# Attention and mixture-of-experts block: one sequence for the score maxima of all units, head-block subtraction on GpSimd

## Chip, cores and metric

The kernel runs on one core of one Trainium2 chip. The metric is device time of one launch in microseconds (us), given as the median of the runs.

## What is computed

The input x has 4 sequences of 2048 rows of 256. It is layer-normalised to xn; the output is x plus two branches of xn.

```python
x = x + attn(xn) + ffn(xn)
# attn: per row, 16 heads of 16 attend to each other (16 x 16 scores a row)
score = jnp.einsum('bsid,bsjd->bsij', Q, K) / jnp.sqrt(jnp.float32(D_K))
attn = jax.nn.softmax(score, axis=-1)
# ffn: causal latent attention over 2048 positions, 16 heads of 16, then top-2 of 8 experts
c = h @ Wdkv
scores = jnp.einsum('bqhd,bkhd->bhqk', q, k) / jnp.sqrt(...)
scores = jnp.where(causal, scores, -1e9)
a = jax.nn.softmax(scores, axis=-1)
out = jnp.einsum('bhqk,bkhd->bqhd', a, v)
```

The first branch is cheap and has no matrix shape: it is done on VectorE and GpSimd in blocks of 128 rows, the "head blocks". The second is the causal attention of this case, then the experts.

## The kernel before

Five stages run one after the other: projections (phase1_project), causal attention (phase2_attend), routing, experts, and the combination. The change is in phase2_attend alone.

**Units and steps.** The attention has 16 units (`UNITS`), each of four heads of one sequence. A unit goes through 40 steps (`STEPS`, L675): for each of four chunks of 512 queries the key tiles of 128 up to the diagonal. In a step TensorE computes transposed scores of two pairs of heads into two PSUM buffers (`scores`, L1109, with masks on the diagonal by `add_mask`, L144), ScalarE takes their exponentials (`exps`, L1036), and two steps later (`LAG`) TensorE multiplies them with the values (`values`, L1127). At the end of a chunk ScalarE copies the result out (`copy_pv`, L1049). On the diagonal a step covers only 384, 256 or 128 of the 512 queries.

**Maxima.** A softmax over transposed scores needs each row's maximum beforehand. It enters the scores as two more rows of the query tile. So while unit n is attended, TensorE also computes the untransposed scores of unit n+1 piece by piece (`score_pair`, L1078, masks L144) into a ring of three PSUM banks, and VectorE reduces every piece to its maximum (`reduce_item`, L971). A pair is two pieces, one of each half of the heads, and takes two banks; a unit has 72 pairs, 144 reductions. A piece is 512 wide in most pairs, 384 in eight, and two heads of 128 or of 256 together in eight. TensorE issues a pair once two banks are free. After the last pair VectorE reduces the piece maxima to negated row maxima (`reduce_maxima`, L978), TensorE transposes them (`transpose_max`, L1092), VectorE splits them in two bf16 parts (`split_maxima`, L986, L988), and SyncE stores them into the next unit's query tile (`store_neg_rows`, L94), which the scores of step 0 wait for.

**Order of work.** It is written out by hand, one program per engine. `PAIRS_BY` says how many pairs are issued by the end of each step: it shares them over steps 0 to 34 by cost, the last `AHEAD` = 5 steps have none, and the last unit has none at all. Per step the pairs are 2 2 2 1 | 3 2 2 2 3 1 2 1 | 3 2 2 2 2 3 2 2 2 2 1 2 | 2 2 2 2 3 2 2 2 2 2 3 0 0 0 0 0 (a bar ends a chunk). In a step TensorE issues both scores, half of the pairs, the values, then the other half. The transpose comes in step 36.

**Head blocks.** GpSimd weighs two head blocks a unit (`weigh_heads`, products at L905, sums at L911, L917, result L924), loads the next two, scores them (`score_heads`, L890 to L898), and divides one tile of attention results by the softmax sums (`divide`, L938). Of each block VectorE takes the maximum and subtracts it (`shift_heads`, L998 and L1000), at steps 12 and 20 (`SHIFT_AT`); ScalarE takes the exponential two steps later (L1043), which `weigh_heads` waits for. VectorE also inverts the sums at step 10 (L993). Semaphores keep each engine's order, so an engine that waits holds all behind it in its program.

**Loads.** There are three slots of unit tiles. SyncE loads unit n+2 in 26 parts, two a step of its own list, each waiting for a later `values` of unit n (up to step 24).

Of the kernel before, what the change touches and what calls it, by code (L numbers as in the profile page):

```python
# [665 lines left out]
def phase2_attend(nc, apart, qk_heads, v_units, o, head_qkv, attn_rows, first_units):  # L666
# [23 lines left out]
    PAIRS_BY = [sum(sum(pair_cost[:m + 1]) * sum(step_cost) <= sum(step_cost[:i + 1]) * sum(pair_cost)  # L690
                    for m in range(N_PAIR)) for i in range(N_STEP)]
    assert PAIRS_BY[N_STEP - AHEAD - 1] == N_PAIR

    with ExitStack() as ctx:
# [14 lines left out]
        piece_max = sb("p2_piece_max", [P, HG, KT, NC])  # L709
# [48 lines left out]
        SHIFT_AT = (12, 20)  # L758
# [7 lines left out]
        N_ITEM = 2 * N_PAIR + 1  # L766
        assert SLOTS * N_ITEM % RING == 0

        MAX_ITEM = N_ITEM - 1

        def ring_item(n, s, r):

            return N_ITEM * n + r, (N_ITEM * s + r) % RING

        def units(eng, body):

            for n in range(UNITS):
                body(n, n % SLOTS, (n - 1) // SLOTS, (n - 1) % SLOTS, n + 1 < UNITS)

        def first(n):  # L780
            return isinstance(n, int) and n == 0

        def next_round(j, k):

            return j + (k + 2) // SLOTS

        @block.sync
        def _(sp):
            def store_neg_rows(n, s):
                wait_apart(sp, ring_free, RING + ring_item(n - 1, 0, MAX_ITEM)[0] + 1, apart)  # L790
                store_neg(sp, q6[s], neg_hi, neg_lo, neg_stored)
# [63 lines left out]
        def _(pool):  # L855
# [7 lines left out]
            nc.gpsimd.memset(piece_max[:, :, :, :], -3e38).then_inc(consts, 1)  # L863
# [23 lines left out]
            def score_heads(m, u, loads, before):  # L887

                wait_apart(pool, head_loaded[u], 16 * loads, apart)
                step(nc.gpsimd.tensor_tensor(  # L890
                    terms[:, :, :, :], head_in[:, u, 0, :, :].unsqueeze(2).to_broadcast([P, H, H, DH]),
                    head_in[:, u, 1, :, :].unsqueeze(1).to_broadcast([P, H, H, DH]), ALU.mult), before + 1)
                width = DH // 2
                for k in range(STEPS_A - 1):
                    step(nc.gpsimd.tensor_tensor(terms[:, :, :, 0:width], terms[:, :, :, 0:width],  # L895
                                                 terms[:, :, :, width:2 * width], ALU.add), before + 2 + k)
                    width //= 2
                nc.gpsimd.tensor_tensor(head_s[:, u, :, :], terms[:, :, :, 0], terms[:, :, :, 1], ALU.add  # L898
                                        ).then_inc(head_scored, 1)
                wait_apart(pool, head_scored, m + 1, apart)  # L900

# [47 lines left out]
            with pool.Fori(1, UNITS - 1) as n:  # L949
                body(n)  # L950
                divide(n - 1)
            for u in range(2):
# [6 lines left out]
        def _(dve):  # L959
# [7 lines left out]
            def reduce_item(m, half, g, bank):  # L967
                h, heads, (i, pc, width) = PAIRS[m]
                h += half * PAIR
                dve.wait_ge(ring_filled, g + 1)  # L970
                nc.vector.tensor_reduce(piece_max[:, h:h + heads, i, pc],  # L971
                                        ring_ps[bank][:, 0:heads * width].rearrange("p (h k) -> p h k", h=heads), AX_X,
                                        ALU.max).then_inc(ring_free, 1)

            def reduce_maxima(n, last_item):

                dve.wait_ge(ring_free, RING + last_item + 1)
                nc.vector.tensor_reduce(neg_max[:, 0:HG * KT], piece_max[:, :, :, :].rearrange("p h i c -> p (h i) c"), AX_X, ALU.max, negate=True  # L978
                                        ).then_inc(neg_max_done, 1)

            def split_maxima(n, g, bank):

# [3 lines left out]
                nc.vector.tensor_copy(neg_hi[:, :], ring_ps[bank][0:HG * KT, 0:P]).then_inc(neg_hi_done, 1)  # L986
                dve.wait_ge(neg_hi_done, n + 1)
                nc.vector.tensor_tensor(neg_lo[:, :], ring_ps[bank][0:HG * KT, 0:P], neg_hi[:, :], ALU.subtract  # L988
# [6 lines left out]
            def shift_heads(m, u):  # L995
# [8 lines left out]
            def body(n, s, j, k, has_next):  # L1004
                done = 0
                for i in range(N_STEP):
                    if i in SHIFT_AT:
                        u = SHIFT_AT.index(i)
                        shift_heads(2 * n + u, u)
                    if i == INVERSE_AT and not first(n):  # L1010
                        invert_sums(n - 1)
                    upto = PAIRS_BY[i] if has_next else 0
                    for m in range(done, upto):
# [4 lines left out]
                    done = upto  # L1018
                    if has_next and i == N_STEP - AHEAD + 1:
                        split_maxima(n + 1, *ring_item(n, s, MAX_ITEM))  # L1020
            units(dve, body)

        @block.scalar
        def _(act):
# [26 lines left out]
            def body(n, s, j, k, has_next):  # L1051
                for i in range(N_STEP):
                    if i - 2 in SHIFT_AT:
                        u = SHIFT_AT.index(i - 2)
# [7 lines left out]
            units(act, body)  # L1062

        @block.tensor
        def _(pe):
            def score_pair(s, m, rnd, g, bank):

                h, heads, (i, pc, width) = PAIRS[m]
                banks = [ring_ps[(bank + half) % RING] for half in range(2)]
                if m == 0:  # L1070
                    pe.wait_ge(loaded[s], N_LOAD * (rnd + 1))
# [17 lines left out]
            def transpose_max(n, g, bank):  # L1089
                pe.wait_ge(neg_max_done, n + 1)  # L1090
                pe.wait_ge(ring_free, g + 1)
                nc.tensor.transpose(ring_ps[bank][:, 0:P], neg_max[:, :], ident[:, :]).then_inc(ring_filled, 1)  # L1092
# [41 lines left out]
            def body(n, s, j, k, has_next):  # L1134
                def maxima(first, end):

                    for m in range(first, end):
                        score_pair((s + 1) % SLOTS, m, next_round(j, k), *ring_item(n, s, 2 * m))

                done = 0  # L1140
                for i in range(N_STEP):
                    scores(n, s, i, 0)
                    scores(n, s, i, 1)
                    upto = PAIRS_BY[i] if has_next else 0
# [5 lines left out]
                    done = upto  # L1150
                    if has_next and i == N_STEP - AHEAD + 1:
                        transpose_max(n + 1, *ring_item(n, s, MAX_ITEM))
                for i in range(N_STEP - LAG, N_STEP):
                    values(n, s, i)
            units(pe, body)
# [909 lines left out]
```

## Time and profile before

| | us |
|---|---|
| median of three runs (3166.71 to 3174.38) | 3169.0 |
| the profiled execution | 3161.7 |
| its span in the profile | 3160.2 |

| engine | busy us | share of the span |
|---|---|---|
| TensorE | 2568.8 | 81% |
| VectorE | 2379.8 | 75% |
| GpSimd | 2236.2 | 71% |
| ScalarE | 1543.0 | 49% |

The profile calls TensorE PE and its weight loads PEld, VectorE DVE, ScalarE ACT, GpSimd POOL; L971 is line 971 of the kernel. A timeline row gives start and length in us, the engine, the line, the operation with output and input, and after x how many instructions were merged; in brackets stands the idle time before it and what ended it. A row by stretches gives the stretch, its length, then busy time and (x) instructions of PE, PEld, DVE, ACT and POOL, the granted clock of TensorE, the DMA share and GB/s. A row by groups gives busy time, mean ns of one, and the idle time before. The attention stage runs from 461 to 2086 us of the span.

### The profile page before, as it was taken

To read this page: it belongs to the slowest core of one execution; us is meant where nothing else is said; L and a number is where in the kernel's file an instruction comes from. 1 tells how busy PE (TensorE), PEld (TensorE's weight loads), DVE (VectorE), ACT (ScalarE), POOL (GpSimd) and SP (SyncE) were. 2 spreads that over 40 slices of the span, in tenths; PEclk is the share of its full clock that TensorE was granted. 3 is DMA by queue.
4 is the path that set the end of the run, shared out by engine and by line. 5 is a ranking of instruction groups with operands and counts; after the bars stand their busy time and mean duration, and the time that the engine had idled before them with its cause. 6 is when DMAs were issued, how large, how long until landed. Compare 5 with 4: busy or idle time off the path is not lost. (4 is left out here: it accounts for less than half of the span.)

```text
span 3160.2 us, 60322 instructions
## 1 busy us (share of the span) xinstructions
PE 2568.8 (81%) x21392; PEld 1318.1 (42%) x21392; DVE 2379.8 (75%) x3812; ACT 1543.0 (49%) x2314; POOL 2236.2 (71%) x1193
## 2 busy tenths in 40 slices
PE   7969978899989998899989998948749888999600
PEld 4534432333233333333233333217638777777500
DVE  4447759888988889888988889305657999999334
ACT  2222216666666666667666666822214444444200
POOL 4433339889888988888888988946746656666376
PEclk9979989999999999999999999977759999999855
DMA  6996542232322233222322220147756666666686
GB/s 195 201 299 200 171 145 63 51 75 80 85 72 62 77 83 78 56 81 79 82 62 75 80 81 24 33 140 245 237 192 220 208 201 201 207 211 206 210 248 203
DMA packets 346974, 435.68 MB, mean 138 GB/s; under 512 B 40859, under 2 KB 276861, under 8 KB 346749
## 3 DMA queue, kind: packets, MB, share of 16 engines
q1 hardware_dynamic: 300796, 350.81, 38.5%
q0 software_dynamic: 17920, 54.55, 5.4%
q10 hardware_dynamic: 28032, 27.27, 2.5%
q8 instruction: 147, 2.41, 0.3%
q14 instruction: 79, 0.64, 0.1%
HBM read 273.43 MB, written 158.47 MB: 137 GB/s over the span
## 5 line engine op out<-in xcount | busy, mean ns | idle before, releaser
L971 DVE TENSOR_REDUCE p_piece_max<-p_ring 128x1 f32<-128x512 f32 (+3 forms) x2160 | 1279.4, 653 | 163.2 <-PE p_ring L144 110.7
L1036 ACT ACTIVATE p_probs<-p_st 128x1024 f32<-128x1024 f32 (+3 forms) x1280 | 1076.7, 894 | 497.6 <-PE p_st L1109 295.6
L1109 PE MATMUL p_st<-unit_q,unit_k 64*128 64x512 bf16 (+3 forms) x3520 | 419.1, 348 | 16.5 <-POOL p_minus_one L869 11.5
L905 POOL TENSOR_TENSOR p_terms<-p_head_p,p_head_in 128x4096 f32<-128x4096 f32 x32 | 347.4, 10856 | 102.0 <-ACT p_head_p L1043 101.7
L1127 PE MATMUL p_pv<-p_probs,unit_vg 128*32 128x512 f32 (+3 forms) x3520 | 409.9, 542 | 0.0
L1739 POOL TENSOR_TENSOR p_pv<-p_pr,p_qkv 128x4096 f32<-128x4096 f32 x32 | 347.4, 10857 | 37.0 <-ACT p_pr L1837 36.4
L1078 PE MATMUL p_ring<-unit_k,unit_q 64*128 64x512 bf16 (+3 forms) x1600 | 273.1, 355 | 101.2 <-DVE p_piece_max L971 100.0
L1910 PE MATMUL p_y_ps<-p_w,p_hid 128*128 128x256 f32 x1152 | 284.1, 403 | 27.6 <-ACT p_hid L1850 27.5
L890 POOL TENSOR_TENSOR p_terms<-p_head_in 128x4096 f32<-128x4096 f32 x32 | 283.0, 8844 | 7.6 <-POOL p_head_s L898 4.4
L1897 PE MATMUL p_hid_ps<-p_rT,p_w 128*128 128x256 f32 x1152 | 263.4, 382 | 3.3 <-issue 2.2
L911 POOL TENSOR_TENSOR p_terms<-p_terms 128x2048 f32<-128x2048 f32 (+2 forms) x96 | 252.7, 2632 | 17.1 <-POOL p_terms L911 11.4
L895 POOL TENSOR_TENSOR p_terms<-p_terms 128x2048 f32<-128x2048 f32 (+2 forms) x96 | 252.0, 2625 | 17.1 <-POOL p_terms L895 11.4
L1910 PEld LDWEIGHTS p_y_ps<-p_w,p_hid 128*128 128x128 f32 x1152 | 227.6, 203 | 66.7 <-ACT p_hid L1850 34.3
L1078 PEld LDWEIGHTS p_ring<-unit_k,unit_q 64*128 64x128 bf16 x1600 | 70.8, 93 | 432.9 <-DVE p_piece_max L971 427.0
L1897 PEld LDWEIGHTS p_hid_ps<-p_rT,p_w 128*128 128x128 f32 x1152 | 219.9, 192 | 35.9 <-issue 5.5
L1109 PEld LDWEIGHTS p_st<-unit_q,unit_k 64*128 64x128 bf16 x3520 | 139.7, 95 | 197.3 <-ACT p_probs L1036 92.2
L1109 PE MATMUL p_st<-p_q,p_k 34*128 34x512 bf16 (+7 forms) x1600 | 188.2, 346 | 0.0
L1127 PE MATMUL p_pv<-p_probs,p_vg 128*32 128x512 f32 (+3 forms) x1600 | 186.3, 542 | 0.0
L1969 POOL DMA_INDIRECT p_ye<-expert_rows,p_pos x128 | 132.6, 1036 | 72.2 <-issue 71.9
L1078 PE MATMUL p_ring<-p_k,p_q 64*128 64x512 bf16 (+3 forms) x800 | 135.6, 352 | 49.7 <-DVE p_piece_max L971 49.1
L1775 DVE TENSOR_TENSOR p_prod<-p_q_ps,p_qkv 128x4096 f32<-128x4096 f32 x32 | 141.5, 4421 | 32.1 <-ACT p_q_ps L1830 32.1
L1384 POOL DMA_INDIRECT sorted_rows<-p_th,p_pos x128 | 134.0, 1047 | 37.5 <-issue 36.3
(194 smaller groups left out, 3603.8 us busy)
## 6 DMA issues: line engine op xcount, KB each, us to landing
p_w<-ffn_w SPq DMA_DIRECT2D x144, 512.0 KB, 5.1
qk_parts<-p_parts SPq DMA_DIRECT2D x64, 384.0 KB, 3.2
head_qkv<-p_heads SPq DMA_DIRECT2D x16, 1536.0 KB, 6.7
p_rows<-sorted_rows SPq DMA_DIRECT2D x72, 256.0 KB, 4.2
expert_rows<-p_y ACTq DMA_DIRECT2D x72, 256.0 KB, 5.6
unit_q<-qk_parts SPq DMA_DIRECT2D x132, 128.0 KB, 3.2
unit_k<-qk_parts SPq DMA_DIRECT2D x132, 128.0 KB, 3.6
p_x<-attn_x SPq DMA_DIRECT2D x32, 512.0 KB, 5.7
```

Of the source, the lines that this page charges most:

```text
L890: step(nc.gpsimd.tensor_tensor(terms[:, :, :, :], head_in[:, u, 0, :, :].unsqueeze(2).to_broadcast([P, H, H, DH]), head_in[:, u, 1, :, :]. ...
L895: step(nc.gpsimd.tensor_tensor(terms[:, :, :, 0:width], terms[:, :, :, 0:width], terms[:, :, :, width:2 * width], ALU.add), before + 2 + k)
L905: step(nc.gpsimd.tensor_tensor(terms[:, :, :, :], head_p[:, u, :, :].unsqueeze(2).to_broadcast([P, H, DH, H]), head_in[:, u, 2, :, :].rear ...
L911: step(nc.gpsimd.tensor_tensor(terms[:, :, :, 0:width], terms[:, :, :, 0:width], terms[:, :, :, width:2 * width], ALU.add), before + 2 + k)
L971: nc.vector.tensor_reduce(piece_max[:, h:h + heads, i, pc], ring_ps[bank][:, 0:heads * width].rearrange("p (h k) -> p h k", h=heads), AX_X ...
L1036: nc.scalar.activation(probs[:, 2 * turn_of(s, i) + u, :, 0:width], st_ps[u][:, :, 0:width], ACT.Exp).then_inc(probs_done, 1)
L1078: last[half] = nc.tensor.matmul(banks[half][:, k * width:(k + 1) * width], q6[s][rows, h + k, i * P:(i + 1) * P], k6[s][rows, h + k, pc * ...
L1109: last = nc.tensor.matmul(st_ps[u][:, half, 0:width], k6[s][rows, PAIR * second + u, kt * P:(kt + 1) * P], q6[s][rows, PAIR * second + u, ...
L1127: last = nc.tensor.matmul(pv_ps[hh * VW:(hh + 1) * VW, skip:CT], vg[s][:, kt, hh * VW:(hh + 1) * VW], probs[:, 2 * turn_of(s, i) + hh % PA ...
L1739: nc.gpsimd.tensor_tensor(pv[:, u, :, :, :], pr[:, u, :, :].unsqueeze(2).to_broadcast([P, H, DH, H]), qkv[:, u, 2, :].rearrange("p (j d) - ...
L1897: last = nc.tensor.matmul(hid_ps[i][:, f * ROW_TILE:(f + 1) * ROW_TILE], w1[:, u, k, (2 * i + f) * P:(2 * i + f + 1) * P], rT[:, k, :], st ...
L1910: last = nc.tensor.matmul(y_ps[t][:, 0:D], hid[:, f, t * P:(t + 1) * P], w2[:, u, f, :], start=f == 0, stop=f == FB - 1)
```

## The change

There is now one sequence of pairs over all units: 72 for each of units 1 to 15, 1080 in all (`TOTAL`), and `ISSUED[n][i]` says how many are issued by the end of step i of unit n. Each unit's pairs are complete at the end of step 33 of the unit before (`AHEAD` = 6), and the last six steps issue the first ten pairs of the unit after. Unit 0 so issues 82 pairs, units 1 to 13 issue 72 each, unit 14 issues 62, unit 15 none. Step costs are weighted so that narrow steps on the diagonal get fewer. In units 1 to 13 the pairs per step are 2 2 1 1 | 2 2 2 2 2 2 1 0 | 2 2 3 2 2 2 2 2 2 2 1 0 | 2 2 2 2 2 3 2 2 2 2 2 2 2 2 1 1.

The piece maxima have two buffers, by the parity of the unit, since pieces of the next unit are written before those of this one are negated. The negation comes after the first pair of the following unit, the transpose and the split after its third (`NEGATED_AT`, `TURNED_AT`); the transposed maxima take one place in the ring there.

VectorE only takes the maxima of the head blocks, at steps 12 and 14 (`HEADS_AT`); GpSimd subtracts them, both blocks ahead of both weighings; ScalarE's exponentials of the head blocks come at steps 14 and 16.

```diff
-    AHEAD = 5
-    skipped = lambda c, kt: max(0, kt - TT * c) * P
-    step_cost = [CT + CT - skipped(c, kt) for c, kt in STEPS[:N_STEP - AHEAD]]
-    pair_cost = [P + 2 * heads * width for _, heads, (_, _, width) in PAIRS]
...
+    AHEAD = 6
+    TOTAL = N_PAIR * (UNITS - 1)
+    diagonal_step = lambda c, kt: kt >= TT * c
+    step_cost = [CT + P // 4 - max(0, kt - TT * c) * P + P // 16 * diagonal_step(c, kt) for c, kt in STEPS]
+    pair_cost = [HALF + heads * width for _, heads, (_, _, width) in PAIRS]
+    STEPS_BY = [sum(step_cost[:i + 1]) / sum(step_cost) for i in range(N_STEP)]
+    PAIRS_BY = [sum(pair_cost[:m + 1]) / sum(pair_cost) for m in range(N_PAIR)]
+    END = STEPS_BY[N_STEP - AHEAD - 1]
+
+    def issued(n, i):
+
+        share = STEPS_BY[i]
+        work = share / END if n == 0 and share < END else n + 1 - END + share
+        whole = int(work + 1e-9)
+        return min(TOTAL, N_PAIR * whole + sum(by <= work - whole + 1e-9 for by in PAIRS_BY))
...
+    NEGATED_AT = [min(N_PAIR * u + 1, TOTAL) for u in range(1, UNITS)]
+    TURNED_AT = [min(N_PAIR * u + 3, TOTAL) for u in range(1, UNITS)]
...
-        piece_max = sb("p2_piece_max", [P, HG, KT, NC])
+        piece_max = sb("p2_piece_max", [P, 2, HG, KT, NC])
...
-        SHIFT_AT = (12, 20)
+        HEADS_AT = (12, 14)
...
+            def shift_heads(m, u):
+                wait_apart(pool, head_max_done, m + 1, apart)
+                nc.gpsimd.tensor_tensor(head_s[:, u, :, :], head_s[:, u, :, :],
+                                        head_max[:, u, :].unsqueeze(2).to_broadcast([P, H, H]), ALU.subtract
+                                        ).then_inc(head_shifted, 1)
...
             def body(n):
                 for u in range(2):
+                    shift_heads(2 * n + u, u)
+                for u in range(2):
                     weigh_heads(2 * n + u, u, n, steps(2 * n + 2, 2 * n + u))
...
-                dve.wait_ge(head_max_done, m + 1)
-                nc.vector.tensor_tensor(head_s[:, u, :, :], head_s[:, u, :, :],
-                                        head_max[:, u, :].unsqueeze(2).to_broadcast([P, H, H]), ALU.subtract
-                                        ).then_inc(head_shifted, 1)
...
+                    for p in range(before_step(n, i), ISSUED[n][i]):
                         for half in range(2):
-                            reduce_item(m, half, *ring_item(n, s, 2 * m + half))
-                    if done < upto == N_PAIR:
-                        reduce_maxima(n + 1, ring_item(n, s, MAX_ITEM - 1)[0])
...
+                            reduce_item(p, half)
+                        if p + 1 in NEGATED_AT:
+                            reduce_maxima(1 + NEGATED_AT.index(p + 1))
+                        if p + 1 in TURNED_AT:
+                            split_maxima(1 + TURNED_AT.index(p + 1))
```

## Rows read from the trace of the kernel before

**Rows 1.** Timeline of VectorE, the first reduction of units 1 and 14.

```profile
571.58 0.76 DVE L971 TENSOR_REDUCE p_piece_max<-p_ring 128x2 f32<-128x256 f32 x2 [6.16 <-PE p_ring L144]
...
1898.33 0.76 DVE L971 TENSOR_REDUCE p_piece_max<-p_ring 128x2 f32<-128x256 f32 x2 [6.16 <-PE p_ring L144]
```

**Rows 2.** Busy time by stretches: 14 units, one unit's first 93 us, its end.

```profile
561.69:1990.40 1428.71, 1289.82 (x14806) 452.49 (x14798) 1247.69 (x2130) 976.89 (x1205) 1225.22 (x518) 1.00 0.27 72
...
1080.99:1174.25 93.26, 83.56 (x916) 28.29 (x916) 88.22 (x150) 62.28 (x76) 79.25 (x37) 0.98 0.31 79
...
1174.25:1184.08 9.83, 9.79 (x149) 4.25 (x141) 0.98 (x3) 7.54 (x12) 9.65 (x2) 1.00 0.08 22
```

**Rows 3.** Waits of the attention stage, 490 to 2085 us: total, times, longest.

```profile
PE p_ring L1078 <- DVE p_piece_max L971: 145.4, 217, 3.0
...
POOL p_terms L905 <- ACT p_head_p L1043: 101.7, 15, 9.4
...
DVE p_piece_max L971 <- PE p_ring L144: 94.1, 42, 6.2
```

**Rows 4.** Timeline of VectorE in one unit, 1330 to 1383 us.

```profile
1338.07 1.48 DVE L1000 TENSOR_TENSOR p_head_s<-p_head_s,p_head_max 128x256 f32<-128x256 f32 x1
...
1350.51 18.27 DVE L971 TENSOR_REDUCE p_piece_max<-p_ring 128x1 f32<-128x512 f32 x30
...
1382.25 0.28 DVE L986 CAST p_neg_hi<-p_ring 64x128 bf16<-64x128 f32 x1 [2.65 <-PE p_ring L1092]
```

**Rows 5.** VectorE's groups of instructions by shape, 561.69 to 1990.4 us.

```profile
L1000 DVE TENSOR_TENSOR p_head_s<-p_head_s,p_head_max 128x256 f32<-128x256 f32 x28 | 26.6, 950 | 1.0
...
L998 DVE TENSOR_REDUCE p_head_max<-p_head_s 128x16 f32<-128x256 f32 x28 | 11.4, 407 | 0.0
...
L993 DVE RECIPROCAL p_inverse<-p_sums 128x64 f32<-128x64 f32 x14 | 7.6, 541 | 0.0
...
L978 DVE TENSOR_REDUCE p_neg_max<-p_piece_max 128x64 f32<-128x256 f32 x15 | 6.3, 420 | 0.5
```

**Rows 6.** Lines L1000, L924 and L905 by themselves: ns min/median/max.

```profile
L1000 DVE TENSOR_TENSOR p_head_s<-p_head_s,p_head_max x32: 424/1450/5604, 495.8 to 2026.6; 128x256 f32<-128x256 f32 x32
...
L924 POOL TENSOR_TENSOR p_head_o<-p_head_o,p_head_inv x32: 619/620/622, 530.4 to 2081.8; 128x256 f32<-128x256 f32 x32
...
L905 POOL TENSOR_TENSOR p_terms<-p_head_p,p_head_in x32: 10817/10848/11072, 505.0 to 2056.3; 128x4096 f32<-128x4096 f32 x32
```

**Rows 7.** Timeline of TensorE: two wide steps, values after a stand, the stage's end.

```profile
1136.80 1.79 PE L1127 MATMUL p_pv<-p_probs,unit_vg 128*32 128x512 f32 x8
...
1159.04 1.03 PE L1109 MATMUL p_st<-unit_q,unit_k 64*128 64x512 bf16 x8
...
1159.99 0.39 PE L1078 MATMUL p_ring<-unit_k,unit_q 64*128 64x512 bf16 x2
...
1160.31 1.06 PE L1127 MATMUL p_pv<-p_probs,unit_vg 128*32 128x512 f32 x8
...
1161.31 0.34 PE L1078 MATMUL p_ring<-unit_k,unit_q 64*128 64x384 bf16 x2
...
2076.46 1.50 PE L1127 MATMUL p_pv<-p_probs,unit_vg 128*32 128x384 f32 x24
```

**Rows 8.** Timeline of SyncE's issues, the last loads of unit n+2.

```profile
1147.20 2.57 SPq L75 DMA_DIRECT2D p_vg<-v_padded  x2
```

**Rows 9.** Timeline of GpSimd, weighings and the last division.

```profile
1116.27 10.84 POOL L905 TENSOR_TENSOR p_terms<-p_head_p,p_head_in 128x4096 f32<-128x4096 f32 x1 [6.73 <-ACT p_head_p L1043]
...
1219.36 10.83 POOL L905 TENSOR_TENSOR p_terms<-p_head_p,p_head_in 128x4096 f32<-128x4096 f32 x1 [7.97 <-ACT p_head_p L1043]
...
1933.60 10.87 POOL L905 TENSOR_TENSOR p_terms<-p_head_p,p_head_in 128x4096 f32<-128x4096 f32 x1 [6.73 <-ACT p_head_p L1043]
...
2028.79 11.07 POOL L905 TENSOR_TENSOR p_terms<-p_head_p,p_head_in 128x4096 f32<-128x4096 f32 x1
...
2083.70 2.35 POOL L938 TENSOR_TENSOR p_raw<-p_raw,p_spread 128x1024 f32<-128x1024 f32 x1
```

More of the change, by code:

```diff
@@ L684, in phase2_attend, with before_step @@
     LAG = 2
-    AHEAD = 5
-    skipped = lambda c, kt: max(0, kt - TT * c) * P
-    step_cost = [CT + CT - skipped(c, kt) for c, kt in STEPS[:N_STEP - AHEAD]]
-    pair_cost = [P + 2 * heads * width for _, heads, (_, _, width) in PAIRS]
-    PAIRS_BY = [sum(sum(pair_cost[:m + 1]) * sum(step_cost) <= sum(step_cost[:i + 1]) * sum(pair_cost)
-                    for m in range(N_PAIR)) for i in range(N_STEP)]
-    assert PAIRS_BY[N_STEP - AHEAD - 1] == N_PAIR
+    AHEAD = 6
[11 more added lines that the diff above has]
+        return min(TOTAL, N_PAIR * whole + sum(by <= work - whole + 1e-9 for by in PAIRS_BY))
+    ISSUED = [[issued(n, i) for i in range(N_STEP)] for n in range(UNITS)]
+    assert all(ISSUED[n][N_STEP - AHEAD - 1] == N_PAIR * (n + 1) for n in range(UNITS - 1))
+    NEGATED_AT = [min(N_PAIR * u + 1, TOTAL) for u in range(1, UNITS)]
+    TURNED_AT = [min(N_PAIR * u + 3, TOTAL) for u in range(1, UNITS)]
+    def before_step(n, i):
+        return ISSUED[n][i - 1] if i else ISSUED[n - 1][N_STEP - 1] if n else 0
     with ExitStack() as ctx:
@@ L764, in phase2_attend, with pair_item, turn_item, units @@
         assert SLOTS * N_STEP % (LAG + 1) == 0
[L766 to L775, printed above, removed]
-            for n in range(UNITS):
[L778 to L785, printed above, removed]
+        def pair_item(p):
+            return 2 * p + sum(at <= p for at in TURNED_AT)
+        def turn_item(u):
+            return 2 * TURNED_AT[u - 1] + u - 1
+        def units(body):
+            for n in range(UNITS):
+                body(n, n % SLOTS)
         @block.sync
@@ L951, in _ @@
                 divide(n - 1)
+            for u in range(2):
+                shift_heads(2 * (UNITS - 1) + u, u)
             for u in range(2):
@@ L1061, in body, with score_pair @@
                 copy_pv(n, NC - 1)
-            units(act, body)
+            units(body)
         @block.tensor
         def _(pe):
-            def score_pair(s, m, rnd, g, bank):
+            def score_pair(p):
+                n, m, g = 1 + p // N_PAIR, p % N_PAIR, pair_item(p)
+                s = n % SLOTS
                 h, heads, (i, pc, width) = PAIRS[m]
-                banks = [ring_ps[(bank + half) % RING] for half in range(2)]
+                banks = [ring_ps[(g + half) % RING] for half in range(2)]
                 if m == 0:
-                    pe.wait_ge(loaded[s], N_LOAD * (rnd + 1))
+                    pe.wait_ge(loaded[s], N_LOAD * (n // SLOTS + 1))
                 pe.wait_ge(ring_free, g + 2)
@@ L1087, in score_pair, with transpose_max @@
                     last[half].then_inc(ring_filled, 1)
[L1089 removed]
+            def transpose_max(n):
+                g = turn_item(n)
                 pe.wait_ge(neg_max_done, n + 1)
                 pe.wait_ge(ring_free, g + 1)
[L1092 removed]
+                nc.tensor.transpose(ring_ps[g % RING][:, 0:P], neg_max[:, :], ident[:, :]).then_inc(ring_filled, 1)
             def scores(n, s, i, u):
@@ L1132, in _, with maxima, body @@
             pe.wait_ge(consts, 2)
[L1134 to L1140, printed above, removed]
+            def maxima(first, end):
+                for p in range(first, end):
+                    score_pair(p)
+                    if p + 1 in TURNED_AT:
+                        transpose_max(1 + TURNED_AT.index(p + 1))
+            def body(n, s):
                 for i in range(N_STEP):
@@ L1149, in body @@
                     maxima(cut, upto)
-                    done = upto
-                    if has_next and i == N_STEP - AHEAD + 1:
-                        transpose_max(n + 1, *ring_item(n, s, MAX_ITEM))
                 for i in range(N_STEP - LAG, N_STEP):
                     values(n, s, i)
-            units(pe, body)
+            units(body)
 ROW_TILE = 256
```

56 lines of the change are left out of this document (26 added, 30 removed).

## The prediction

> **What bounds the kernel now.** I read first where the change acts. The attention stage works through 16 units of 40 steps; a unit repeats itself to a few hundredths of a microsecond, so one can be read for all. Its start is the first reduction of two 256-wide pieces: from unit 1 to unit 14 that is (1898.33 - 571.58) / 13 = 102.06 us a unit [rows 1]. Most last 101.86, two last 103.1.
>
> Then the busy times of stretches [rows 2]. Of 102.05 us (1428.71 / 14) TensorE is busy 92.13, VectorE 89.12, GpSimd 87.52, ScalarE 69.8. No engine is full, and three are close, so the loss is in how they fit. The stretch of one unit up to the negated maxima has VectorE busy 88.22 of 93.26 and TensorE 83.56; in the last 9.83 us, which hold steps 35 to 39, VectorE has 0.98 us of work and TensorE 9.79. So 35 steps run at VectorE's pace while TensorE waits, and five at TensorE's while VectorE waits. The waits say the same [rows 3]: over this stage TensorE waits 145.4 us for a free bank (9.9 a unit), VectorE 94.1 us for the first piece of a unit. GpSimd waits 101.7 us for the head blocks' exponentials.
>
> VectorE's own rows [rows 4] give the price of a piece: a run of 30 reductions takes 18.27 us, about 0.60 each, 1.20 a pair. The subtraction of a head block took 1.48 there and 424 to 5604 ns over the units, for one shape [rows 6], so VectorE is sometimes held by something, most likely GpSimd, which is always at work there.
>
> **The change, part by part.**
>
> (a) *One sequence through all 40 steps.* I price a step by the larger of TensorE's and VectorE's share. TensorE [rows 7]: scores 0.95 (1159.04 to 1159.99), values 1.00 (1160.31 to 1161.31), a pair 0.23 ahead of scores and 0.32 ahead of values, 0.275 on average; for 384, 256 and 128 columns the starts in the same view give scores of 0.78, 0.57 and 0.34 and values of 0.79, 0.60 and 0.38; a masked score of 512 is 1.00, a pair's mask adds 0.06. VectorE: 1.20 a full pair, 0.94 at 384 columns, 0.66 at 2 x 128. With the pair counts of both schedules the excess of VectorE over TensorE is, before, 0.21, 0.57, 0.16, 0.70, 0.40, 0.72, 0.28, 0.70, 0.52, 0.32, 0.07, 0.72, 0.52, 0.83 and 0.70 (steps 0, 1, 2, 4, 5, 8, 10, 12, 13, 17, 21, 23, 25, 28, 34): 7.4 us. After: 0.73, 1.07, 0.30, 0.40, 0.07, 0.18, 0.52, 0.32, 0.30, 0.52, 0.32 and 0.07 (steps 0, 1, 4, 5, 9, 12 to 14, 24, 25, 29, 37): 4.8 us. TensorE's total is the same. The 7.4 and VectorE's 3.3 us of head blocks and reciprocal ((26.6 + 11.4 + 7.6) / 14, [rows 5]) make 10.7 where 9.9 are measured, so the tally is slightly harsh. Part (a) is worth **2.6 us** a unit, not the 9 us of the idle stretch: TensorE is full there, and each pair moved in lengthens it.
>
> (b) *Subtractions off VectorE.* 26.6 / 14 = 1.90 us a unit, in steps where VectorE is the later engine: I take all, **1.9 us**; it would be nothing where TensorE covers them.
>
> (c) *The unit's end.* Negating (0.42, [rows 5]) and splitting (0.28 and as much again, [rows 4]) used to lie in the idle stretch and now sit between pairs of steps 34 to 36. There TensorE has 2.60, 2.48 and 2.67 against VectorE's 1.86, 1.88 and 2.40: hidden; uncovered it would be 1.0. The 2.65 us wait for the transpose now comes two pairs later than the negation, behind other reductions: nothing. The stores of the negated maxima, on SyncE's queue ahead of the next unit's scores, gain about one step of lead. The two buffers cost a memset of 256 more elements on GpSimd ahead of everything, near 0.2 us once. Pieces of unit n+2 need its loads by step 34: the last two are issued from 1147.20 [rows 8], step 34 comes past 1169. SyncE's order does not change otherwise.
>
> So the TensorE and VectorE loop goes from 101.86 to 101.86 - 2.6 - 1.9 = **97.4**.
>
> (d) *Subtractions on GpSimd.* Its chain from the first weighing to the end of the division takes 1219.36 - 7.97 - 1116.27 = 95.12 us; then it waits, 7.97 here and 6.73 in most units [rows 9]. The nearest row is the product of the same shape, 620 ns [rows 6]; two are 1.24, and with 0.18 to 0.36 of gap the chain is **96.7**. All of it lay behind the wait; now little is left: 97.4 against 96.7. The Trainium skill, "GPSIMD Engine Reference", section 3.1, puts tensor_tensor on GpSimd at 1.96 times VectorE, which on 0.42 would be 0.82 each and 0.4 us a unit more; the 620 ns row is for this shape on this engine and decides.
>
> (e) *New waits.* GpSimd's second subtraction waits for VectorE's step 14; behind it stand both weighings, their stores and the next loads. ScalarE's step 14 waits for the first subtraction, behind it all exponentials and so TensorE's scores. While GpSimd is not the last, this costs the first weighing about 1 us once. Two loops 0.7 us apart, tied at two points, will not mesh perfectly: I add 0.2 and take **97.6 us a unit**.
>
> (f) *The ends.* Unit 0 takes 10 pairs more: its steps 14 to 39 go from 63.7 to 68.2 by the tally, unit 1's first 14 from 33.0 to 30.5, and 1.9 comes off; the first interval between weighings stays near 101.9. The stage ends with GpSimd: last weighings from 2028.79, division until 2086.05 [rows 9], TensorE's last values until 2078 [rows 7]. That chain of 57 us stays.
>
> **The sum** by the start of the first weighing: unit 0 at 505.0 + 1 = 506; unit 1 at 607.9; 13 units of 97.6 give 1876.7 for unit 14 (now 1933.60); the last interval, with a light last unit, is GpSimd's 97: 1973.7 against 2028.79. **55 us less.** The stages behind do not change. The profiled execution has a span of 3160.2 and a time of 3161.7; the median of the runs is 3169.0, 7 us above. I take 55 off the median: **3114 us**.
>
> Bounds: with both loops at GpSimd's 96.7 from the start, 15 x (102.04 - 96.7) less 1 to 5 gives about 77 less, 3092. If neither (a) nor the fit holds, 100 us a unit, 22 less, 3147. A difference below 0.3% (9.5 us) can't be told from none.
>
> **Rivals.**
>
> *GpSimd becomes the bound.* For: only 6.7 us of slack, and the loop's branch has always lain behind that wait, so no row prices it. Against: the other gaps of its chain are 0.18 to 0.36. With 2 us more the unit is 98.7 and the gain 55 - 14 x 1.1 = 40: 3129. Chance 0.2.
>
> *Spreading brings nothing.* For: TensorE is 9.79 of 9.83 busy in the stretch that receives work, and three banks hold one and a half pairs, so VectorE starves behind a 1.00 us values block. Against: the run of 30 reductions without a break [rows 4] shows two pairs a step being fed. Then only (b) is left: 100 us a unit, the gain 13 x 2.1 = 27: 3142. Chance 0.12. The Trainium skill says, in "Perfetto Trace Analysis", section "Optimizing Scalar/DVE Operations", that VectorE and GpSimd share a read port, so that moving work between them might not help. By that rule (b) would vanish and (a) stay, much the same time; against it, GpSimd's large products last 10817 to 11072 ns beside a VectorE that is full and beside one that is idle [rows 6].
>
> *Slower.* At step 14 VectorE, ScalarE and TensorE are tied to GpSimd: VectorE waits for the second scores, then GpSimd divides (2.35) and subtracts (1.24) before ScalarE may take its step (69.8 / 40 = 1.7). If these 5.3 us are added to each unit rather than covered, TensorE stands for more than 2.6 us; after such a stand the same values took 1.79 instead of 1.06 [rows 7] and that unit 103.1 instead of 101.86, 1.2 more. 97.4 + 5.3 + 1.2 = 103.9 a unit, 1.9 x 15 = 28 more: 3197. It decides once GpSimd's second scores come later than VectorE's step 14 and its chain exceeds 102.06, 5.4 above my price. Against: the whole chain ends at 1211.39, division and all, and ScalarE's step 14 comes at 1219. Chance 0.06.
>
> That the pieces aren't spread (a late load, a bank that is not free) would leave (b) alone; it is in the second rival.
>
> **How the numbers follow.** Forecast 0.62, rivals 0.2, 0.12 and 0.06. The first three are all below 3160. For steps I did not foresee I take some off: faster 0.87, same 0.06, slower 0.07. The range holds forecast, the first two rivals and the bounds, save a little at either end: 3092 to 3143.
>
> **What would show it.** Units 97 to 98.5 us apart; VectorE without the 6 us gap at a unit's start; TensorE busy about 92 of 97.6; its wait for banks down from 9.9 to about 5 us; GpSimd's wait ahead of L905 down from 6.7 to under 1.5; two GpSimd subtractions of 0.62. Wrong would be: a wait of ScalarE for subtractions of several microseconds a unit, a lower granted clock around step 14, a wait ahead of the new pieces for loads, or units still above 100.

## The result and the profile after

The changed kernel takes 3125.3 us (median of four runs, 3123.49 to 3126.2) against 3171.6 of the kernel before in the same comparison: a ratio of 0.9855, 95% interval [0.9838, 0.9872], 46 us less. The prediction said 3114, range 3092 to 3143, faster. The profiled execution has a time of 3123.49 and a span of 3122.0; the table below takes it against the one before.

| us | before | after |
|---|---|---|
| unit 0's first weighing starts at | 505.00 | 508.62 |
| from there to unit 1's | 101.85 | 103.69 |
| the next 13 intervals, mean | 102.06 | 98.45 |
| the last interval | 95.19 | 96.53 |
| unit 15's first weighing to the last division's end | 57.26 | 57.03 |

The first row is 3.6 later because the stage began later in this execution, 460.98 instead of 457.40, before any changed instruction; counted from the stage's start it is 47.64 against 47.60. From its start to its last division the stage takes 1584.7 instead of 1628.7: **44 us less**, where 55 were forecast.

GpSimd's timeline gives all rows of that table (start, length, line, what was computed, idle time before it in brackets with its releaser). A weighing begins at L917, formerly L905 [rows 9]; the subtractions are L910, the division L950.

```profile
508.62 10.83 POOL L917 TENSOR_TENSOR p_terms<-p_head_p,p_head_in 128x4096 f32<-128x4096 f32 x1
...
612.31 10.92 POOL L917 TENSOR_TENSOR p_terms<-p_head_p,p_head_in 128x4096 f32<-128x4096 f32 x1
...
1102.29 0.62 POOL L910 TENSOR_TENSOR p_head_s<-p_head_s,p_head_max 128x256 f32<-128x256 f32 x1
1104.48 0.62 POOL L910 TENSOR_TENSOR p_head_s<-p_head_s,p_head_max 128x256 f32<-128x256 f32 x1 [1.56 <-DVE p_head_max L1015]
1105.06 10.89 POOL L917 TENSOR_TENSOR p_terms<-p_head_p,p_head_in 128x4096 f32<-128x4096 f32 x1
...
1203.05 10.91 POOL L917 TENSOR_TENSOR p_terms<-p_head_p,p_head_in 128x4096 f32<-128x4096 f32 x1
...
1891.55 0.62 POOL L910 TENSOR_TENSOR p_head_s<-p_head_s,p_head_max 128x256 f32<-128x256 f32 x1 [3.14 <-DVE p_head_max L1015]
1892.13 10.90 POOL L917 TENSOR_TENSOR p_terms<-p_head_p,p_head_in 128x4096 f32<-128x4096 f32 x1
...
1988.66 10.85 POOL L917 TENSOR_TENSOR p_terms<-p_head_p,p_head_in 128x4096 f32<-128x4096 f32 x1
...
2043.34 2.35 POOL L950 TENSOR_TENSOR p_raw<-p_raw,p_spread 128x1024 f32<-128x1024 f32 x1
```

Nine of the 13 intervals last 97.98 to 98.01 us (1203.05 - 1105.06 is one), one 99.18 and three about 99.57. The 6.73 us wait for ScalarE [rows 9] is gone; in its place stands a wait of 1.56 ahead of the second subtraction, and of 3.14 where a unit is long. GpSimd's own chain is therefore 97.99 - 1.56 = 96.43 us.

By stretches: 14 units, and five microseconds of a long unit (columns as in [rows 2]).

```profile
568.00:1941.00 1373.00, 1279.24 (x14739) 451.45 (x14735) 1215.71 (x2092) 973.28 (x1201) 1232.89 (x539) 1.00 0.28 74
1301.04:1306.04 5.00, 5.00 (x38) 1.26 (x36) 3.17 (x7) 1.55 (x3) 5.00 (x2) 0.66 0.00 0
```

Of 98.07 us a unit TensorE is now busy 91.4, VectorE 86.8, GpSimd 88.1. VectorE has lost 2.3 us against [rows 2]. Not all of that is the subtraction: this stretch also holds ten pairs fewer, since unit 14 issues 62.

The waits of the attention stage (490 to 2045 us: total, times, longest):

```profile
PE p_ring L1090 <- DVE p_piece_max L988: 98.3, 209, 1.3
DVE p_piece_max L988 <- PE p_ring L1090: 96.2, 95, 2.1
DVE p_piece_max L988 <- PE p_ring L144: 56.7, 100, 1.5
POOL p_head_s L910 <- DVE p_head_max L1015: 36.4, 15, 6.1
...
ACT p_head_p L1053 <- POOL p_head_s L910: 8.3, 2, 4.9
```

TensorE's wait for banks fell from 145.4 [rows 3] to 98.3, 7.0 a unit. VectorE's longest wait for a piece fell from 6.2 to 2.1 us. The waits for masked pieces (L144) fell from 94.1 to 56.7 in all, but those for pieces without a mask rose from 33.2 to 96.2: the idle time at a unit's start has not gone, it is spread over the steps. ScalarE waits for a subtraction twice in the whole stage.

VectorE's timeline around the weighing and around the turn from one unit to the next:

```profile
1195.17 0.41 DVE L1015 TENSOR_REDUCE p_head_max<-p_head_s 128x16 f32<-128x256 f32 x1
1197.09 4.87 DVE L988 TENSOR_REDUCE p_piece_max<-p_ring 128x2 f32<-128x512 f32 x8 [1.51 <-PE p_ring L144]
1201.88 0.41 DVE L1015 TENSOR_REDUCE p_head_max<-p_head_s 128x16 f32<-128x256 f32 x1
...
1253.60 0.41 DVE L995 TENSOR_REDUCE p_neg_max<-p_piece_max 128x64 f32<-128x256 f32 x1
1254.38 2.22 DVE L988 TENSOR_REDUCE p_piece_max<-p_ring 128x2 f32<-128x512 f32 x4 [0.37 <-PE p_ring L144]
1256.51 0.27 DVE L1003 CAST p_neg_hi<-p_ring 64x128 bf16<-64x128 f32 x1
```

The negation and the split have no gap before them: the 2.65 us wait of [rows 4] is gone. The second head maximum (1201.88) is what GpSimd's second subtraction waits for; it starts at 1202.47.

### The profile page after: what moved, and what is told of

Same layout as the page of the kernel before. It is cut to its first block and busy times, and to the rows that moved or that the text cites. A ratio compares the mean times of both kernels' runs of the same rounds, so it can differ in the third digit from the quotient of the medians.

```text
span 3122.0 us, 60368 instructions
## 1 busy us (share of the span) xinstructions
PE 2562.5 (82%) x21392; PEld 1316.3 (42%) x21392; DVE 2338.2 (75%) x3780; ACT 1543.6 (49%) x2314; POOL 2254.1 (72%) x1225
## 5 line engine op out<-in xcount | busy, mean ns | idle before, releaser
L917 POOL TENSOR_TENSOR p_terms<-p_head_p,p_head_in 128x4096 f32<-128x4096 f32 x32 | 347.6, 10861 | 0.4
L615 PE MATMUL p_heads_ps<-p_wh,p_hT 128*128 128x512 f32 x256 | 126.6, 617 | 44.3 <-DVE p_heads L469 44.3
```

The source lines that it names most:

```text
L917: step(nc.gpsimd.tensor_tensor(terms[:, :, :, :], head_p[:, u, :, :].unsqueeze(2).to_broadcast([P, H, DH, H]), head_in[:, u, 2, :, :].rear ...
```

## The experiments

Four first runs take the change apart and shift the balance of the two loops; five more follow up what they left open. Each was timed beside the kernel before on the same chip: that one's median was 3171.1 for the first four, 3170.5 for the next three, 3168.7 for the last two. The unit lengths are distances of weighings as above.

**One sequence alone.** The subtraction goes back to VectorE, head blocks at steps 12 and 20 as before.

```diff
-        HEADS_AT = (12, 14)
+        HEADS_AT = (12, 20)
...
-                    shift_heads(2 * n + u, u)
...
+                dve.wait_ge(head_max_done, m + 1)
+                nc.vector.tensor_tensor(head_s[:, u, :, :], head_s[:, u, :, :], ..., ALU.subtract)
```

> The changed kernel with the head blocks' subtraction put back on VectorE, at steps 12 and 20; the one sequence of pairs stays. Theory (TensorE and VectorE set the unit, the sequence is worth 2.6 us a unit and the subtraction 1.9): units of 98.0 + 1.9 = 99.9 us, 15 x 1.9 = 28 us above the changed kernel, about 3153. Rival (spreading the pairs brings nothing, since TensorE is full in the stretch that receives them): units stay at 101.9, about 3170. Rival (the subtraction brings nothing): units of 98.0, about 3125.

Measured: 3151.6 us, ratio 0.9938 [0.9922, 0.9955]. Most units last 99.88, so the sequence alone is worth 101.86 - 99.88 = 1.98 us a unit. In GpSimd's timeline it waits for ScalarE, as before:

```profile
1117.05 10.86 POOL L911 TENSOR_TENSOR p_terms<-p_head_p,p_head_in 128x4096 f32<-128x4096 f32 x1 [5.38 <-ACT p_head_p L1047]
```

This refutes the rival by which spreading brings nothing. The subtractions that went back to VectorE did not come back at their old price, though. Its group of them over 14 units (576 to 1960 us), and one of them in its timeline above what GpSimd ran at the time:

```profile
L1007 DVE TENSOR_TENSOR p_head_s<-p_head_s,p_head_max 128x256 f32<-128x256 f32 x28 | 43.0, 1537 | 1.0
...
1210.45 2.05 DVE L1007 TENSOR_TENSOR p_head_s<-p_head_s,p_head_max 128x256 f32<-128x256 f32 x1
...
1209.86 2.36 POOL L944 TENSOR_TENSOR p_raw<-p_raw,p_spread 128x1024 f32<-128x1024 f32 x1 [0.36 <-POOL p_head_s L904]
```

They take 43.0 / 14 = 3.07 us a unit instead of 1.90 [rows 5]: with the pairs spread, the one at step 12 meets GpSimd's division (the last section shows how). So the 1.98 us are what the sequence brings while the subtractions cost 1.17 more.

**The subtraction alone.** The kernel before with its own pairs per step, GpSimd subtracting, head blocks at steps 12 and 14.

```diff
-        SHIFT_AT = (12, 20)
+        SHIFT_AT = (12, 14)
...
+                nc.gpsimd.tensor_tensor(head_s[:, u, :, :], head_s[:, u, :, :], ..., ALU.subtract)
```

> The kernel before with the subtraction on GpSimd alone, head maxima at steps 12 and 14; the pairs keep their old steps. Theory: 101.86 - 1.9 = 100.0 us a unit, 15 x 1.9 = 28 us less than before, about 3143. Rival (TensorE covers VectorE's subtraction): 101.5 or more, about 3168. Rival (the new tie at step 14 costs what the subtraction gave): unchanged or above 3172, with ScalarE waiting for the subtraction.

Measured: 3150.5, ratio 0.9936 [0.9919, 0.9952]. A unit is 100.41: 1.45 us less than before, where 1.9 were expected. In the timelines of GpSimd and of VectorE:

```profile
1115.33 0.62 POOL L904 TENSOR_TENSOR p_head_s<-p_head_s,p_head_max 128x256 f32<-128x256 f32 x1 [4.04 <-DVE p_head_max L1008]
```

```profile
1179.65 0.76 DVE L981 TENSOR_REDUCE p_piece_max<-p_ring 128x2 f32<-128x256 f32 x2 [6.16 <-PE p_ring L144]
```

The idle stretch at a unit's start is whole, 6.16 us as in [rows 1], and the unit is shorter all the same, so a shorter unit did not need that gap filled. The two parts sum to 3.43, together they bring 101.86 - 97.99 = 3.87. Taken in the prediction's order the sequence brings 1.98 and then the subtraction 1.89; in the other order the subtraction brings 1.45 and then the sequence 100.41 - 97.99 = 2.42 (the second head maximum moves from step 20 to 14 with the subtraction in both readings).

The first interval is 103.77 here, with the old pairs, close to the change's 103.69, but not for the same reason: here the granted clock is 0.50 from 510 to 515 us, where the change has 1.00. With the sequence alone, which has no tie at step 14, the first interval is 105.85, with the clock at 0.50 again (507.5 to 512.5 us). No run singles out what the change lost there.

**GpSimd longer.** Four additions of 512 elements ahead of the subtractions, in every unit but the last.

```diff
             def body(n):
+                for k in range(4):
+                    nc.gpsimd.tensor_tensor(spare[:, 1 + k, :], spare[:, 0, :], spare[:, 0, :], ALU.add)
                 for u in range(2):
                     shift_heads(2 * n + u, u)
```

> The changed kernel with four additions of 512 elements (1.04 us each, about 4.1 in all) put into GpSimd's chain ahead of the subtractions of every unit. Theory (GpSimd has only the 1.56 us that it waits for the second head maximum): chain 96.4 + 4.1 = 100.5, units from 98.0 to 100.5, about 14 x 2.5 + 4 = 39 more, 3164. Rival (GpSimd already sets the unit): 4.1 more a unit, 62 in all, 3187. Rival (GpSimd has more room than its wait shows): under 15 more.

Measured: 3158.9, ratio 0.9961 [0.9947, 0.9975], 100.47 us a unit, as the theory said; the total is 5 us below its 3164.

```profile
1117.19 4.02 POOL L956 TENSOR_TENSOR p_spare<-p_spare 128x512 f32<-128x512 f32 x4
1121.18 1.19 POOL L912 TENSOR_TENSOR p_head_s<-p_head_s,p_head_max 128x256 f32<-128x256 f32 x2
1122.42 10.86 POOL L919 TENSOR_TENSOR p_terms<-p_head_p,p_head_in 128x4096 f32<-128x4096 f32 x1
...
1222.86 10.87 POOL L919 TENSOR_TENSOR p_terms<-p_head_p,p_head_in 128x4096 f32<-128x4096 f32 x1
```

```profile
ACT p_head_p L1057 <- POOL p_head_s L912: 54.3, 15, 6.9
```

The unit is 1222.86 - 1122.42 = 100.44 to 100.47, the 96.43 of GpSimd's chain plus the additions' 4.02 to 4.04. Its wait for the head maximum is gone from ordinary units, and ScalarE now waits for it 54.3 us in all. Only 2.5 of the 4 us reached the unit: the other 1.5 were GpSimd's slack.

**Reductions over half of each piece.** VectorE reads half of the columns, and the exponentials are scaled by 0.01 so that they stay finite: maxima and softmax are not the reference's here.

```diff
-   ...rearrange("p (h k) -> p h k", h=heads), AX_X,
+   ...rearrange("p (h k) -> p h k", h=heads)[:, :, 0:width // 2], AX_X,
-   ... ACT.Exp)
+   ... ACT.Exp, scale=0.01)
```

> The changed kernel with every piece reduced over half its columns, and the exponentials of the scores scaled by 0.01 so that they stay finite: the softmax of the attention is not the reference's. VectorE's 144 reductions a unit fall from 0.60 to about 0.33 each. Theory (VectorE and TensorE set the unit by turns, GpSimd's chain of 96.4 lies right behind): units fall to 96.5 and no further, 15 x 1.5 = 22 less than the changed kernel, about 3102. Rival (GpSimd is not close): units near TensorE's 91.5 to 93, about 3045. Rival (TensorE alone sets the unit): 98.0 stays.

Measured: 3093.2, ratio 0.9759 [0.9743, 0.9776]. GpSimd's timeline, and the busy times of 800 us:

```profile
1087.30 1.21 POOL L910 TENSOR_TENSOR p_head_s<-p_head_s,p_head_max 128x256 f32<-128x256 f32 x2
1088.55 10.82 POOL L917 TENSOR_TENSOR p_terms<-p_head_p,p_head_in 128x4096 f32<-128x4096 f32 x1
...
1185.03 10.90 POOL L917 TENSOR_TENSOR p_terms<-p_head_p,p_head_in 128x4096 f32<-128x4096 f32 x1
```

```profile
700.00:1500.00 800.00, 755.02 (x8720) 267.03 (x8714) 446.16 (x1238) 577.27 (x713) 737.40 (x325) 0.97 0.29 78
```

With VectorE busy 56% instead of 89% of the time, the unit shortens by only 1.5 us, to 96.5, and stops there because GpSimd no longer waits for any other engine from unit to unit. That is the floor that the change has built: 96.4. The total is 9 us below the expected 3102; no unit is lengthened as four were in the change, and the first interval is 97.61, so the ten pairs more and the tie together cost no more than 1.1 us there once VectorE's reductions are short. ScalarE waits for its subtraction 71.0 us in this run, so here the loop is held by the tie from the other side.

**Pairs spread by hand.** The weights that give `ISSUED` leave steps with three pairs and steps with none. A list written out gives nearly every wide step two.

```diff
+    PLAN = (1, 1, 2, 1, 2, 2, 2, 2, 2, 2, 1, 1, 1, 2, 2, 2, 2, 2, 2, 2,
+            2, 2, 2, 1, 2, 1, 2, 2, 2, 2, 2, 2, 2, 2, 2, 2, 2, 2, 2, 2)
...
+        return min(TOTAL, N_PAIR * n + TAIL + sum(PLAN[:i + 1]))
```

> The changed kernel with the pairs per step written out so that VectorE's share exceeds TensorE's in as few steps as possible (1 1 2 1 | 2 2 2 2 2 2 1 1 | 1 2 2 2 2 2 2 2 2 2 2 1 | 2 1 and then 2 to the end): by the tally of the prediction, with VectorE's other work put in its steps, the excess falls from 7.8 to 3.9 us a unit. Theory (TensorE and VectorE set the unit by the step, and GpSimd's chain of 96.5 stands right behind, as the run with half reductions showed): 96.5 a unit, 15 x 1.5 plus the clock's dips at step 14, 25 less than the changed kernel, 3100. Rival (the tally says nothing about single steps, the banks smooth them out): 98.0, 3125. Rival (GpSimd is no bound here): 94.1, 3067.

Measured: 3110.5, ratio 0.9815 [0.9798, 0.9831]. Units alternate between 96.8 and 97.7, mean 97.3, where 96.5 and 3100 were expected. From GpSimd's timeline, two units in turn:

```profile
1097.79 0.62 POOL L919 TENSOR_TENSOR p_head_s<-p_head_s,p_head_max 128x256 f32<-128x256 f32 x1 [0.49 <-ACT p_head_p L1062]
...
1195.43 0.62 POOL L919 TENSOR_TENSOR p_head_s<-p_head_s,p_head_max 128x256 f32<-128x256 f32 x1 [1.31 <-DVE p_head_max L1024]
```

GpSimd's slack is down to 0.5 to 1.3 us. TensorE's wait for banks is 52.2 instead of 98.3, so the list does to the pairs what it should. That the near floor hides the rest is my reading; the next runs take the floor away.

**Head sums on VectorE.** To lower the floor, VectorE takes the head blocks' sums and their reciprocal, five GpSimd instructions a block less, with either list of pairs.

```diff
-                    step(nc.gpsimd.tensor_tensor(head_sum..., ALU.add), before + 5 + k)
-                step(nc.gpsimd.tensor_tensor(head_inv[:, :], head_sum[:, :, 0], minus_one[:, :], ALU.pow), before + 9)
...
+        SUMS_AT = (17, 19)
+                nc.vector.tensor_reduce(head_sum[:, u, :], head_p[:, u, :, :], AX_X, ALU.add)
+                nc.vector.reciprocal(head_inv[:, u, :], head_sum[:, u, :])
```

> The changed kernel with the sums of the head blocks' exponentials and their reciprocals taken from GpSimd (five instructions, about 5.2 us with their gaps, for each of two blocks) and given to VectorE at steps 17 and 19 (a reduction of 0.41 and a reciprocal of about 0.15 each). Theory (GpSimd is not the bound at 98.0): GpSimd's chain falls to 86 and gives nothing; VectorE's 1.1 us more are partly covered: 98.0 to 99.1 a unit, 3125 to 3140. The end of the stage, which is GpSimd's, gets about 10 us earlier until TensorE's end stands in its way (3.7 us earlier at present), so 4 less: 3121 to 3136. Rival (GpSimd is the bound): units well under 98, 3110 or less.

> Both together. Theory: with GpSimd's chain at 86 the even pairs can give all: 98.0 - 3.9 + 1 = 95.1 a unit, 15 x 2.9 = 43 less than the changed kernel and 4 at the end, 3078. Rival (the banks smooth the steps out): as the changed kernel, 3121 or above. Rival (the tally overstates by half): 97, 3106.

Measured: 3127.8, ratio 0.9865 [0.9849, 0.9882], units of 98.83 with the change's pairs; 3105.3, ratio 0.9804 [0.9786, 0.9822], units of 97.63 with the list. GpSimd now waits 183.1 us in the first (two waits in most units, 6.27 and 6.09 us in one of them), so it is nowhere near the bound, and the unit is still 0.84 longer than the change's 97.99. VectorE got 1.3 us of work (two sums of 0.41, two reciprocals of 0.25), it seems in steps where it is the later engine, which the next two runs try. The second was expected at 95.1 and came 2.5 above it, at the rival by which the tally overstates (97 a unit, 3106): with GpSimd far from the bound in both, the list brings 98.83 - 97.63 = 1.2 us where the tally has 3.9.

**The same sums in steps 22 and 23**, the end of a chunk, where the tally gives VectorE room. Against the list above, the second run's also has one pair instead of two in step 22 and two instead of one in step 25, so that its third chunk ends in 1 1 (the expectation says step 23, which had one already).

```diff
-        SUMS_AT = (17, 19)
+        SUMS_AT = (22, 23)
```

> The run with the head blocks' sums on VectorE, with the sums moved from steps 17 and 19 (two pairs each) to steps 22 and 23 (one pair and none). Theory (VectorE's other work costs where its step is full and is free where TensorE has the larger share): units from 98.83 back to 98.0, 15 x 0.83 = 12 less than with the early sums, 3116. Rival (each 1.3 us of work on VectorE costs 0.8 wherever it stands): 98.83, 3128.

> Even pairs with the sums at steps 22 and 23, and one pair in step 23 instead of step 25. The early sums cost 0.83 us a unit with the uneven pairs; if they cost the same with the even ones, 97.63 - 0.8 = 96.8 a unit, 12 less than with the early sums, 3093. Rival (with even pairs something else, such as TensorE's own 92 us and its waits for exponentials, holds the unit at 97.6): 3105.

Measured: 3117.5, ratio 0.9841 [0.9824, 0.9857], units of 97.98 (two of 99.55); and **3090.6, ratio 0.9755 [0.9739, 0.9772], units of 96.45**. With the change's pairs the same instructions cost 0.85 us less by their place alone. With the list the unit falls by 1.18 (97.63 to 96.45), place and moved pair together; no run separates them. Between these two runs the list brings 97.98 - 96.45 = 1.5 us. The last kernel is 78 us below the kernel before, where the change is 46 below. GpSimd's timeline and the busy times:

```profile
1090.10 0.62 POOL L921 TENSOR_TENSOR p_head_s<-p_head_s,p_head_max 128x256 f32<-128x256 f32 x1 [5.08 <-DVE p_head_max L1020]
1095.48 0.62 POOL L921 TENSOR_TENSOR p_head_s<-p_head_s,p_head_max 128x256 f32<-128x256 f32 x1 [4.76 <-DVE p_head_max L1020]
1096.06 10.87 POOL L928 TENSOR_TENSOR p_terms<-p_head_p,p_head_in 128x4096 f32<-128x4096 f32 x1
...
1192.51 10.90 POOL L928 TENSOR_TENSOR p_terms<-p_head_p,p_head_in 128x4096 f32<-128x4096 f32 x1
```

```profile
700.00:1480.00 780.00, 740.65 (x8554) 258.45 (x8548) 716.57 (x1245) 563.63 (x699) 644.93 (x233) 1.00 0.30 79
```

The unit is as short as the one with half reductions, but here it isn't GpSimd's floor: GpSimd has 9.8 us to spare. TensorE is busy 91.6 of 96.45, VectorE 88.6. What holds the last 4.9 us apart was not taken further.

## Why the prediction was right, and where its sizes were off

The unit fell from 101.86 to 97.99 where 97.6 was forecast, with both mechanisms as described. The stage gave 44 us of the 55. Between the first weighings of unit 0 and unit 15 the prediction had 1467.7 us, the profile has 1988.66 - 508.62 = 1480.0. The 12.3 us between them are:

| | us |
|---|---|
| 13 units at 97.99 instead of 97.6 | 5.1 |
| four units lengthened, the clock lowered in each | 5.9 |
| first interval 103.69 instead of 101.9 | 1.8 |
| last interval 96.53 instead of 97 | -0.5 |

The first weighing came 1 us earlier than forecast, which leaves 11.3. Behind the stage, this execution spends 2.1 us more up to its end, and the medians differ by 46.3 where the two stages differ by 43.9; that much the single executions vary.

**(a), the sequence: 2.6 forecast, 1.98 measured alone, 2.42 measured on top of the subtraction.** Part of the shortfall of the first reading is no fault of the sequence: VectorE's subtractions grew from 1.90 to 3.07 us in that run. What failed is the per-step tally, as the later runs show better: for the hand-written list it had 3.9 us, and 1.2 came with the early sums and 1.5 with the late ones and one pair moved. It takes each step's larger share as the step's length, as if the two engines met at the end of every step. I read it so that within a step they meet at every pair, since only three banks lie between them; that is argued, no run tried more banks. The tally also can't tell where in a step VectorE's side work falls, which is worth 0.85 us in the one pair of runs that differ by nothing else. The forecast of TensorE's wait, "down from 9.9 to about 5", is 7.0; the tally's own 4.8 left out the maxima of the head blocks and the reciprocal, 0.8 and 0.5 us, which VectorE keeps.

**(b), the subtraction: 1.9 forecast, 1.89 measured** on top of the sequence, 1.45 without it. The close agreement is luck. The forecast was VectorE's busy time in the old schedule, 1.90, of which 1.45 came; beside the new pairs the same two instructions took 3.07, of which 1.89 came. In both schedules part of the work was covered, the condition that the prediction had named, though it then took all. By what, no run shows; TensorE's own work is the likely cover. The Trainium skill, "Perfetto Trace Analysis", section "Optimizing Scalar/DVE Operations", warns that moving work from VectorE to GpSimd may not help, as they share a read port. Here it helped, by 1.45 to 1.89 us a unit.

**(c), the unit's end: nothing, measured nothing.** Negation and split have no gap before them, no piece waits for its loads, and the memset takes 0.52 us instead of 0.30.

**(d), GpSimd's chain: 96.7 forecast, 96.43 measured.** Each subtraction takes 618 to 630 ns, the 620 of the nearest row [rows 6]; where neither waits, two take 1.19 to 1.21 with no gap between them, and the forecast had 0.18 to 0.36 for gaps on top. The Trainium skill, "GPSIMD Engine Reference", section 3.1, measured its ratio of 1.96 at 2048 elements; an estimate from it would have made it 0.82 each, and for this shape the trace does not agree. The run with longer GpSimd work and the run with shorter reductions enclose the value: 100.47 less 4.04, and 96.5 as the floor.

**(e), the ties: 0.2 forecast.** No run has this term by itself: (a), (b) and (e) together were 4.3 and came as 3.87. The first interval lost 1.8 us against the forecast; the runs leave open how much of that is the tie and how much the ten pairs. A lowered clock around step 14 was named as a sign of failure and priced at 1.2 us in a rival, with nothing for it in the forecast; it came there in three units, at 1.6 each, and in a fourth at another place, at 1.2. The rival tied it to a stand of more than 2.6 us. That was a misreading: the row behind the 1.79 us of values [rows 7] has TensorE idle for 1.56 us, and the 2.6 are the distance between two starts.

```profile
1135.28 0.39 PE L1078 MATMUL p_ring<-unit_k,unit_q 64*128 64x512 bf16 x2 [1.56 <-DVE p_piece_max L971]
```

**(f), the ends:** the chain of 57 us stays, as said. One slip in the range: the prediction counts 100 us a unit as 22 us less in its bounds (3147) and as 27 less in its second rival (3142).

**The rivals.** "GpSimd becomes the bound" did not decide, by 1.6 us, but the room is as small as it was put: longer work on GpSimd comes through after 1.56 us, and faster reductions gain nothing after 1.5 us. "Spreading brings nothing" is refuted by the sequence alone. "Slower" needed several microseconds of ScalarE waiting per unit; it waits twice, 8.3 us in all.

## What to carry to other kernels

An idle stretch of one engine is not the gain of filling it: 6 us of idle stood at each unit's start, filling it gave 2.0 to 2.4, and a kernel with the gap untouched got 1.45 from elsewhere. When two engines hand work over through few buffers, spread the work evenly, and put side work of the tighter engine where the other is slow: two reductions and two reciprocals moved by four and five steps were worth 0.85 us a unit. Price a move by its rows in the schedule that it will meet, not in the old one: the same two subtractions took 1.90 us before and 3.07 beside the new pairs. Before adding work to an engine that waits, work out its whole chain; with 1.6 us left between the two loops, the next gain needs both shortened together.

## What the runs showed of the hardware

**The clock after a short stand.** In TensorE's timeline the wait before the diagonal pairs of step 14 is 1.13 us in each of units 1 to 14, and what follows differs. Two of them, and at the end a row from the start of unit 3:

```profile
1202.95 0.34 PE L1090 MATMUL p_ring<-p_k,p_q 64*128 64x384 bf16 x2 [1.13 <-DVE p_piece_max L988]
...
1203.27 1.07 PE L1140 MATMUL p_pv<-p_probs,unit_vg 128*32 128x512 f32 x8
...
1300.94 0.43 PE L1090 MATMUL p_ring<-unit_k,unit_q 64*128 64x384 bf16 x2 [1.13 <-DVE p_piece_max L988]
...
1301.41 1.94 PE L1140 MATMUL p_pv<-p_probs,p_vg 128*32 128x512 f32 x8
...
780.67 1.81 PE L1140 MATMUL p_pv<-p_probs,unit_vg 128*32 128x512 f32 x8
```

Eight matmuls take 1.94 instead of 1.07, and over the five microseconds from 1301.04 the granted clock is 0.66, so part of it lies at the lower of the two levels (1.2 GHz). The unit comes out at 99.58. The same happened in three of these 14 units (1.93 or 1.94 us for the eight matmuls), after the same wait as in the eleven others (1.06 or 1.07). The fourth long interval, 99.18, has its lower clock elsewhere, in the first steps of unit 3, after waits of 0.78 and 0.80 us: 1.81 in the last row. In the kernel before, a wait of 1.52 to 1.58 us stands at step 20 in all of units 0 to 14, and the lower clock followed it in two, the two units of 103.1. What picks them, the traces don't show. No unit was lengthened so in the runs with the list and the sums on VectorE (97.63 and 96.45 throughout); in the last kernel the pair at this place (1190.88 in its TensorE timeline) starts with no wait at all.

**VectorE beside GpSimd.** One instruction on VectorE varies, its subtraction with both inputs in SBUF: by itself, in the run with one sequence alone, its shortest, median and longest are

```profile
L1007 DVE TENSOR_TENSOR p_head_s<-p_head_s,p_head_max x32: 424/1477/4008, 501.4 to 2010.5; 128x256 f32<-128x256 f32 x32
```

The spread is not chance. That run and the kernel before have 64 of these subtractions. The 16 that begin while GpSimd runs nothing take 0.42 to 0.43 us. The other 48 begin beside a GpSimd instruction, and every one of them ends 0.27 to 0.30 us after that instruction does: the one at 1338.07 [rows 4] ends at 1339.55, and GpSimd's addition from 1336.92 at 1339.27; the longest, 5.60 us, waited out a product of 8.85. So the subtraction is held until GpSimd is done with what it is running. In the kernel before, step 12 of units 1 to 14 fell in GpSimd's wait for ScalarE and cost 0.42 or 0.43, and step 20 of units 0 to 14 fell in its additions and cost 1.44 to 1.50; the wait of TensorE at step 20 above ends one reduction after that subtraction.

```profile
1336.92 2.35 POOL L911 TENSOR_TENSOR p_terms<-p_terms 128x1024 f32<-128x1024 f32 x1 [0.18 <-POOL p_terms L911]
```

The split's second part, of nearly the same kind but with one input in PSUM, takes 282 to 284 ns in all units, though in the kernel before it lies beside a GpSimd product of 8.8 to 8.9 us every time. The Trainium skill, "GPSIMD Engine Reference", section 1, names two SBUF inputs as a case in which VectorE contends with GpSimd, and the trace agrees. On GpSimd the same subtraction never took over 0.63 us in the change's run. An instruction of VectorE like this one is priced by what GpSimd runs at that moment: here 0.42 us beside an idle GpSimd, and otherwise what is left of GpSimd's instruction and 0.28 more. A median over all of them hides that.
